# A transformer decoder on one core: the focused query/key/value stage written as a block of its own, and a weight fold made inside the linear attention

## What is computed

```
    q = _norm_last(jax.nn.relu(q) + EPS)
    k = _norm_last(jax.nn.relu(k) + EPS)
    q = _norm_last(q ** FOCUS)          # FOCUS = 3, _norm_last divides by the sum over a head's 16 values
    k = _norm_last(k ** FOCUS)
    kv = jnp.einsum('bhnd,bhne->bhde', k, v)
    z = 1.0 / (jnp.einsum('bhnd,bhd->bhn', q, k.sum(axis=2)) + EPS)
    out = jnp.einsum('bhnd,bhde,bhn->bhne', q, kv, z)
...
    query = jnp.einsum('bqi,ih->bqh', image_features, Wq) + bq
    key = jnp.einsum('bkt,th->bkh', text_features, Wk) + bk
    scores = jnp.einsum('bqh,bkh->bqk', query, key) * scale
```

## Time and profile before

| | us |
|---|---|
| median of 3 runs | 1926.78 (1926.78 to 1926.79) |
| the profiled execution | 1926.66 |
| its span, first to last instruction | 1923.7 |
| PE busy | 1703.9 (89%) |
| DVE busy | 1592.5 (83%) |
| ACT busy | 1365.9 (71%) |
| POOL busy | 343.0 (18%) |
| mean granted TensorE clock | 0.947 of 2.4 GHz |

### The profile page before, as it was taken

One profiled execution on the slowest core, in us unless ns is written; L12 is line 12 of the kernel. 1 busy time (PEld: TensorE's weight loads), 2 busy tenths in 40 slices (PEclk: granted clock), 3 DMA queues, 4 the chain that ended last, 5 costly groups with the idle time before them and its releaser, 6 DMA issues. The chain is left out here.

```text
span 1923.7 us, 39202 instructions
## 1 busy us (share of the span) xinstructions
PE 1703.9 (89%) x15104; PEld 697.0 (36%) x15104; DVE 1592.5 (83%) x2275; ACT 1365.9 (71%) x2642; POOL 343.0 (18%) x599
## 2 busy tenths in 40 slices
PE   7958989999999999998999999999889787689972
PEld 3512222332332233233222222222254355467761
DVE  3898999989989998887999999999568686677657
ACT  3707979889889988987889999999823254344542
POOL 0910111211021111102101001010035424200004
PEclk9957999999999999999999999999989898899995
DMA  4000000000000000200000000000020000000001
GB/s 128 1 1 1 2 1 2 2 2 2 2 2 1 2 2 1 89 2 1 2 2 2 2 1 2 2 2 2 2 77 1 1 0 1 1 1 2 1 1 44
DMA packets 12689, 18.62 MB, mean 10 GB/s; under 512 B 1856, under 2 KB 10560, under 8 KB 12256
## 3 DMA queue, kind: packets, MB, share of 16 engines
q1 hardware_dynamic: 11664, 14.78, 2.3%
q10 hardware_dynamic: 848, 1.38, 0.2%
HBM read 14.07 MB, written 2.10 MB: 8 GB/s over the span
## 5 line engine op out<-in xcount | busy, mean ns | idle before, releaser
L907 DVE TENSOR_REDUCE mxp<-ps_m 128x2 f32<-128x1024 f32 (+1 forms) x960 | 1088.5, 1188 | 93.1 <-PE ps_m L710 91.2
L842 ACT ACTIVATE work<-ps_s 128x512 f32<-128x512 f32 x1856 | 1010.8, 599 | 134.6 <-PE ps_s L723 86.7
L737 PE MATMUL ps_av<-work,vst 128*32 128x256 f32 x7424 | 596.1, 393 | 11.7 <-ACT avs L849 11.1
L710 PE MATMUL ps_m<-k_stack,qa 48*128 48x512 f16 (+1 forms) x2048 | 380.4, 369 | 24.3 <-DVE mxp L907 23.7
L723 PE MATMUL ps_s<-qb,k_stack 50*128 50x512 f16 x1856 | 366.0, 384 | 30.8 <-ACT work L842 24.9
L737 PEld LDWEIGHTS ps_av<-work,vst 128*32 128x32 f32 x7424 | 147.9, 108 | 346.8 <-ACT work L842 258.8
L723 PEld LDWEIGHTS ps_s<-qb,k_stack 50*128 50x128 f16 x1856 | 109.8, 93 | 423.0 <-ACT work L842 406.6
L710 PEld LDWEIGHTS ps_m<-k_stack,qa 48*128 48x128 f16 x2048 | 105.9, 95 | 67.0 <-DVE mxp L907 56.5
L568 POOL TENSOR_SCALAR mtmp<-negm 128x16 f32<-128x16 f32 x32 | 8.2, 255 | 531.6 <-DVE negm L912 531.4
L822 ACT COPY qb<-ps_s 128x1024 f16<-128x1024 f16 x32 | 32.6, 1020 | 48.2 <-PE ps_s L662 48.2
L1983 ACT CAST oph<-ops_p 128x512 f16<-128x512 f32 x64 | 30.8, 506 | 34.9 <-PE ops_p L1896 34.7
(11 more groups left out here) (363 smaller groups left out, 2099.2 us busy)
## 6 DMA issues: line engine op xcount, KB each, us to landing
x_res<-in_x SPq DMA_DIRECT2D x4, 512.0 KB, 14.0
w_experts<-in_w_experts SPq DMA_DIRECT2D x1, 2048.0 KB, 7.7
out<-x_res SPq DMA_DIRECT2D x8, 256.0 KB, 2.1
v_rows<-in_ctx_c SPq DMA_DIRECT2D x1, 1664.0 KB, 12.6
ctx_n<-in_ctx_n SPq DMA_DIRECT2D x1, 1248.0 KB, 7.5
work<-in_ctx_t SPq DMA_DIRECT2D x1, 784.0 KB, 11.5
w_qkv<-in_w_qkv ACTq DMA_DIRECT2D x1, 768.0 KB, 11.3
w_qkv<-in_w_qkv SPq DMA_DIRECT2D x1, 768.0 KB, 4.3
```

What stands on the lines that cost most here:

```text
L710: m = pe.matmul(ps_m[:, b, e, col:col + width], qa[n % 3][e * HALF:e * HALF + MAXROWS, j, a, :], STACKS[g][e * HALF:e * HALF + MAXROWS, gr ...
L737: m = pe.matmul(ps_av[32 * h:32 * h + 32, cols], vst[n % 2][:, t, h, :], pbuf[(tau[n] + t) % 2][:, h, cols], start=(t == 0 and half == 0), ...
L842: a.activation(pbuf[g % 2][:, h, :], ps_s[:, b, :], ACT.Exp, scale=factor).then_inc(s["exp"], 1)
L907: v.tensor_reduce(dst, src, AX.X, ALU.max).then_inc(s["mred"], 1)
```

## The change

Three things are done. `focused_qkv` no longer calls `linear`: it is one block with all 16 tiles written out, the row normalisation is on ACT, relu and EPS are one DVE instruction, and the first norm is gone (`a` is cubed as it is). The key part is scaled before the query part on POOL. `one_head_setup` is gone as a block: its PE and DVE instructions are spread over steps 0 to 5 of `linear_attention`, in the banks of `ps_kv` that lie idle until step 7, and the ACT instruction is cut in two, in steps 1 and 2. The first projection waits in addition for the last of these DVE instructions (`FOLDED`).

```
+        @block.tensor
...
+            def project(n):
+                pe.wait_ge(s["xt"], n + 1)
+                if n >= 2:
+                    pe.wait_ge(s["relu"], n - 1)
+                    pe.wait_ge(s["vout"], n - 1)
+                for k in range(2):
+                    m = pe.matmul(prod[n % 2][:, 0, :], xt[n % 2][:, k, :], w[:, k, 0:2 * D], start=(k == 0), stop=(k == 1))
+                m.then_inc(s["qk"], 1)
+                for k in range(2):
+                    m = pe.matmul(prod[n % 2][:, 1, 0:D], xt[n % 2][:, k, :], w[:, k, 2 * D:3 * D], start=(k == 0), stop=(k == 1))
+                m.then_inc(s["vv"], 1)
...
+            turn_x(0)
+            for n in range(STEPS):
+                if n + 1 < T:
+                    turn_x(n + 1)
+                if n < T:
+                    project(n)
+                if 0 <= n - 3 < T:
+                    outer(n - 3)
...
+        @block.scalar
+        def _(e):
+            def rows(n):
...
+                e.activation(xn[n % RING][:, :], x[:, n, :], ACT.Identity, bias=nmr[:, n:n + 1], scale=rstd[:, n:n + 1])\
+                 .then_inc(s["xn"], 1)
...
+            for n in range(T):
+                if n + 1 < T:
+                    turned(n + 1)
+                if n + RING - 1 < T:
+                    rows(n + RING - 1)
+                squared(n)
+                value(n)
+
+        @block.vector
+        def _(v):
+            def relu(n):
+                v.wait_ge(s["qk"], n + 1)
+                if n >= 2:
+                    v.wait_ge(s["sq"], n - 1)
+                    v.wait_ge(s["cube"], n - 1)
+                v.tensor_scalar(a[n % 2][:, :, :], heads(prod[n % 2][:, 0, :]), 0.0, EPS_FOCUS, ALU.max, ALU.add).then_inc(s["relu"], 1)
+
+            def third(n):
+                v.wait_ge(s["sq"], n + 1)
+                if n >= 2:
+                    v.wait_ge(s["q"], n - 1)
+                v.tensor_tensor(cube[n % 2][:, :, :], square[n % 2][:, :, :], a[n % 2][:, :, :], ALU.mult).then_inc(s["cube"], 1)
+                v.wait_ge(s["cube"], n + 1)
+                v.tensor_reduce(sums[n % 2][:, :], cube[n % 2][:, :, :], AX.X, ALU.add).then_inc(s["sums"], 1)
+                v.wait_ge(s["sums"], n + 1)
+                v.reciprocal(rs[n % 2][:, :], sums[n % 2][:, :]).then_inc(s["rs"], 1)
+
+            v.scalar_tensor_tensor(nmr[:, :], mean[:, :], -1.0, rstd[:, :], ALU.mult, ALU.mult).then_inc(s["rows"], 1)
+            for n in range(T + 1):
+                if n < T:
+                    relu(n)
+                if n > 0:
+                    third(n - 1)
...
+            for n in range(T):
+                g.wait_ge(s["rs"], n + 1)
+                if n >= RING:
+                    g.wait_ge(s["kv"], n - RING + 1)
+                share(n, 1, k_ring[n % RING][:, :], s["k"])
+                share(n, 0, qf[:, n, :], s["q"])
...
+                if k == 0:
+                    pe.wait_ge(s["fold"], FOLDED)
...
+            def folded(n):
+                if n < 2:
+                    for j in range(2):
+                        m = pe.matmul(ps_f[:, n, :], wq_t[:, j, n * P:n * P + P], wk_t[:, j, :], start=(j == 0), stop=(j == 1))
...
+                for k, some in enumerate((slice(0, 7), slice(7, TM))):
+                    if n == 1 + k:
+                        a.activation(vh[:, some, :], ctx_n[:, some, :], ACT.Copy, scale=ctx_gain[:, 1:2]).then_inc(s["vh"], 1)
...
+                if n == 5:
+                    v.wait_ge(s["made"], 4)
+                    f(v.tensor_scalar(bound[:, :], ps_w[:, 0:1], float(D), None, ALU.mult))
+                    f(v.tensor_copy(wf_peak[:, :], ps_w[:, 2:3]))
+                    f.wait()
+                    f(v.tensor_scalar(bound[:, :], ps_w[:, 1:2], bound[:, :], 1.0 / 16.0, ALU.add, ALU.mult))
+                    f.wait()
+                    power_scale(v, f, bound[:, :], floor[:, :], scale[:, :], back[:, :])
+                    f(v.tensor_scalar(fold[:, :, :], ps_f[:, :, :], scale[:, 0:1], 1.0 / 16.0, ALU.mult, ALU.mult))
```

More of the change, by code:

```diff
@@ L1483, in second @@
-        def second(v, n, r):
-            p = r % 2
-            c = Counted(v, s_cube.sem, 3 * n + s_cube.ahead)
-            v.wait_ge(s_norm, n + 1)
-            v.wait_ge(s_sq, n + 1)
-            s_late.wait(v, 2 * (n - 1))
-            c(v.tensor_tensor(cube[p][:, :, :], square[p][:, :, :], a[r][:, :, :], ALU.mult))
-            c.wait()
-            c(v.tensor_reduce(sums2[:, :], cube[p][:, :, :], AX.X, ALU.add))
-            c.wait()
-            c(v.reciprocal(rs2[p][:, :], sums2[:, :]))
-            c.wait()
@@ L1530, in focused_qkv, with sb @@
-        linear(prog, T, ln_rows(x, mean, rstd), w, 3 * D, epilogue, 2, ident, side=side, late=late, beside=(beside, 3),
-               second=second, side_end=lambda act: squares(act, T - 1, (T - 1) % UNROLL))
-def linear_attention(prog, x, st, qf, ps_kv, tap, tap_bias, w, bias, mask, ident):
+        def sb(name, shape):
+            return cx.enter_context(nc.sbuf_tensor(name, shape, F32))
+        xn, xt = [sb(f"qxn{r}", [P, D]) for r in range(RING)], [sb(f"qxt{p}", [P, 2, P]) for p in range(2)]
@@ new lines, in focused_qkv @@
+        a, square, cube = ([sb(f"q{k}{p}", [P, 2 * H, HD]) for p in range(2)] for k in ("a", "square", "cube"))
+        sums, rs = ([sb(f"q{k}{p}", [P, 2 * H]) for p in range(2)] for k in ("sum", "rs"))
+        nmr = sb("qnmr", [P, T])
+        v_ring, k_ring = [sb(f"qv{r}", [P, 2, P + 1]) for r in range(RING)], [sb(f"qk{r}", [P, D]) for r in range(RING)]
+        turn = [cx.enter_context(nc.psum_tensor(f"qturn{p}", [P, 512], F32)) for p in range(2)]
+        prod = [cx.enter_context(nc.psum_tensor(f"qprod{p}", [P, 2, 512], F32)) for p in range(2)]
@@ L1598, in _ @@
                     turn_o(n - 1)
+                folded(n)
                 for k in range(T):
```

246 lines of the change are left out of this document (110 added, 136 removed).

## The result

The changed kernel takes 1899.82 us (median of 4 runs, 1898.93 to 1901.87), the kernel before 1926.78. The ratio is 0.9862, with a 95% interval from 0.9851 to 0.9874: faster by 1.4%, 27.0 us. The prediction was 1903.1 us, with a range from 1898 to 1909. The profiled execution took 1901.87 us with a span of 1900.0 us. It is the longest of the four, with a mean granted clock of 0.948 where the other three have 0.950 and spans 1.8 to 2.9 us shorter. So a ledger made from it shows less gain than the median does, and what it shows of the clock may be more than in the other three.

What follows compares the result with a forecast made beforehand. DVE was taken to bound the steady focused stage. Focused stage -17.4, fold's block -11.3 and linear attention +5.1 gave -23.6 us, from 1926.66 to 1903.1 us; range 1898 to 1909, eight in ten.

Steps and rivals of the forecast that it cites:

- The steady tiles: Focused stage, steady part: PE becomes the bound, 3.38 us a tile instead of 4.32; twelve tiles gain 11.3 us.
- The relu: Focused stage: relu on DVE takes 0.74 us; between 0.60 and 1 us it hides under PE either way.
- Rival (a): Focused stage: DVE sets the pace, POOL's 1.3 us on its path; 3.9 us a tile, 1909.3 us; chance 0.13.
- Start and end of the stage: Focused stage: 0.7 us gained before the first projection, 5.4 us from the last projection to the next stage.
- The fold's block: Behind the linear attention: with this block gone, DVE's first instruction after it starts earlier, gain 11.3 us.
- The fold in the linear attention, up to the first window: PE's additions cost 4.0 us net, DVE's step 5 1.0, ACT's tenths the rest: +5.1 us.
- The chain of step 5: Linear attention, DVE: 2.33 us of dependent instructions against 1.31 us of idle time, so 1.0 us sticks out.
- Whatever is late here stays late: Linear attention: 5 us late from the first window on, all later steps at their old distances.
- what would make the prediction wrong: Linear attention's later part, where nothing moves, changes its length by over 2 us through the clock.
- rival (b): Linear attention: fold better hidden, PE holding the high clock through the stage's border; 3.5 us less, 1899.6 us; chance 0.22.
- Rival (c): Linear attention: the fold costs its full price, its 11.3 us move rather than vanish; 1909.3 us; chance 0.08.
- Rival (d): Focused stage: instructions of the written-out block come late, kernel slower than before (1935 at 2 us a tile); chance 0.02.

Runs made afterwards that it cites:

- the short chain: Changed kernel with constants in place of the five DVE instructions that make the scale in step 5 of the linear attention: 1901.51 us.
- the kernel before with dummies: Kernel before, plus useless matmuls in the linear attention only, three at its start and three ahead of each window wait: 1927.36 us.
- The doubled products: Changed kernel with each half of the fold's weight product made twice in steps 0 and 1 of the linear attention: 1900.69 us.
- with dummies the median fell by 3.5 us: Changed kernel plus useless matmuls ahead of window waits, at the focused stage's end and at the linear attention's start: 1896.30 us.
- the two short chains: Changed kernel with constants for the scale, 1901.51 us; the same with the one-column product also written with a column scalar, 1898.12 us.

## Why the prediction was right, and where it was off

**The steady tiles.** Right in mechanism: DVE was the bound and PE is the next. The term was 1.8 us too small, -11.3 against -13.1. PE alone takes 2.80 us a tile (two projections without an outer product start at 1539.22 and 1542.02), against 2.83 that I had. The outer product adds 0.45 and not 0.55 us to that (1547.40 to 1547.85): I had read its time to the next turn from a row where it had just waited. 2.80 + 0.45 = 3.25 us is what most tiles took; 12 x (3.38 - 3.25) = 1.6 of the 1.8 us. The gain itself is DVE's load: with the norm back the cadence is 4.09 us in the new block, without it 3.24 us in the old loop.

**The relu.** 0.69 us on DVE, inside the bounds, and hidden: DVE waits 17.7 us for PE.

**Rival (a), POOL on DVE's path.** It did not happen. The mean of the cube is 0.70 us against 0.68 before. Cubes that lost time beside POOL's scaling stand only in the first tiles (0.82 us at 1544.55, 0.95 at 1547.35). The order kept them apart, as argued. In the earlier trace rows I had read a hold that is only in part. Set side by side, the rows say otherwise. The product of the earlier trace rows lost 0.25 us where POOL had 0.39 still to run, the cube at 1547.35 lost 0.27 of 0.40, and the column of the short chain lost 0.81 of 0.97. Each time some 0.15 us less was lost than POOL had left, be the instruction long or short, so each was held to the end of POOL's instruction. The Trainium skill's rule (SBUF — State Buffer, SBUF: two separate sides) is that whichever of two such instructions starts first has the shared port pair for its whole length; these rows agree with it but for those 0.15 us. What saved the forecast was the order, not a milder rule.

**Start and end of the stage.** -0.8 and -6.1 against -0.7 and -5.4. Of the 0.7 us at the end, 0.2 are DVE's last rounds (the last keys ended at 1590.23, 6.7 us behind the last projection's start, where I had 6.9) and 0.5 the way from there to the next stage, 1.1 us instead of the 1.6 that I had carried over from the earlier trace rows.

**The fold's block.** -11.3, exact, with the cross attention starting behind the layer norm as forecast.

**The fold in the linear attention, up to the first window.** +5.8 against +5.1. The turn of tile 3's output (the fourth) stood 8.41 us behind the stage's start before and 13.31 now, +4.9, where I had 4.0. PE's additions took 1.71, 1.27 and 2.20 us to the next turn, 5.2 in all against my 4.9. I had taken the 1.55 us of a pair from the earlier trace rows as its time at the low level; in the kernel before with dummies, with that block at a granted 0.50 throughout, the two pairs took 3.54 us start to start, 1.77 each. The larger error is the 0.9 us of PE's idle time that I let them fill: only 0.3 was filled. The doubled products, which put the window 1.7 us later, show that this is order on PE and not a chance. The chain of step 5 was taken at 1.0 us; it costs 0.83 to 0.87, both from the changed kernel (5.8 - 4.9) and from the kernel without it.

**Behind the first window.** The step that failed: "Whatever is late here stays late", with every later distance unchanged. The part grew by 3.9 us, 0.5 in the window itself and 3.4 behind it. The 0.5 us are POOL again: the first half of DVE's window took 1.30 us instead of 0.79, since one of POOL's additions to `x_res`, 0.72 us long, began 0.02 us after it; the second half took 1.21 us in both. I had named this as what would make the prediction wrong (over 2 us through the clock), and it did happen; it was covered by the steady tiles, the stage's end and the 2.2 us ahead of the stage and behind it, which had nothing to do with the change. That the clock has a part in it is shown and not only argued: at full clock the linear attention takes 50.75 us with the fold and 46.09 without. So of the 9.7 us between the two profiled executions, 4.7 are the fold's work and 5.0 go with the clock. The 5.0 are those of the slowest of four executions of the changed kernel; with dummies the median fell by 3.5 us. The linear attention was some 2 us longer behind a shorter focused stage alone, in a stage of which no instruction was changed (49.74 us behind the new block, 49.52 behind the old loop without the norm); that is one execution of each, and the medians do not bear it out.

**The total.** The median, 1899.82, is inside the range of 1898 to 1909, but 3.3 us below the sum and just outside the 1900.5 to 1906.5 that I had given 0.55. It falls on the 1899.6 of rival (b), whose cause did not occur in the trace. The sum of the profiled executions, -23.7 against -23.6 us, is luck: errors of 4.6 us one way and 4.8 the other, 2.2 of them from outside the change.

**Rival (b), high clock through the border.** I gave it 0.22, and in this kernel it did not happen: the head of the stage is at 0.79 against 0.80 in the kernel before's. With dummies at the border it does (1.00), and the first window starts 2.75 us earlier; the 3.5 us that I had set against it were not worked out beyond 1.4 for step 0.

**Rival (c)** would have had the fold's cost move whole, 11.3 us; at the same clock it is 4.7. **Rival (d)**, late instructions in the written-out block, has nothing for it: PE is busy in all of 41.80 us.

**What stays open.** What puts the clock where it is in the linear attention is not settled beyond this: it moved with how PE was occupied before, and dummies in waits of 0.6 to 2.1 us, at the border and inside, held it up, while those inside alone did so only in part (0.82 in the middle of that stage). Why the same kind of wait (2.12 us) is followed by a slow projection in one kernel and a fast one in the other was not found. How the clock runs in the executions that were not profiled is known only as a mean. Nor was it told apart how much of the 3.4 us between the two short chains is clock.

## What to carry to other kernels

When an engine is nearly full in a steady stage, take its work away first and ask about the loop later: the removed norm gave 11.8 of the 13.1 us of steady gain in the old loop too, and the written-out block was worth its ends. Work that moves from a block of its own into idle places of a neighbour costs what it adds in order to the engine that the others wait for (4.7 of 11.3 us here). Idle time inside such a stage should be counted as filled only where it stands right at the inserted work: of 1.8 us here, 0.3 was. A stage whose PE waits in short pieces can get longer or shorter through the clock with no instruction changed, so compare granted clocks before explaining a few us, and try dummy products at the waits, measured by the median of the whole kernel, since a won level can be given back one block later.

## What the runs showed of the hardware that I had not expected

- The same linear attention had different granted clocks behind different stages: 47.42 us (0.80, 0.90, 1.00 in its thirds), 49.74 us (0.76, 0.81, 0.90), 49.52 us (0.73, 0.82, 0.90) and, with dummies, 46.09 us (1.00). Each is one execution.
- With dummies in the linear attention, the block behind it ran at 0.50 and 0.53 instead of 0.67 and was longer by 2.2 and 1.6 us (15.48 and 14.90 against 13.30), though PE stood idle between them for as long as before.
- A DVE product of one column with two SBUF operands was held for 0.8 us by a POOL product; the same product with the second operand as a scalar per row was not held at all (0.20 us).
- The first projection of the focused stage took 4.09 us in the profiled kernel before, but 5.44 and 5.45 in three other traces of the same loop, for the same matmuls, 3.4 to 3.5 us behind the layer norm's end in all. In two of the three the stage is that of the kernel before, so the norm has nothing to do with it, and the ledger's row of the three tiles ahead of the steady ones would show a gain of 1.3 us against either.
- A DVE instruction with two SBUF operands lost some 0.15 us less than POOL's instruction had left to run, in every row read here (0.12 to 0.16 us in five rows).
